# Idle TensorE products placed by the fill of a stretch instead of by single gaps, in a one-core block of attention, feed-forward and a state-space scan

## The reference, cut to what matters

```python
x = x + _L0_attn_a_ref(_layernorm(x, axis=-1), ...)   # 16 heads of 8, window of 32 and every 64th
x = x + _L0_ffn_ref(_layernorm(x, axis=-1), ...)      # 256 -> 512 -> 512 -> 128, weights +1 or -1
x = x + _L0_attn_b_ref(_layernorm(x, axis=-1), ...)   # 256 channels x 16 states, h = dA * h + dt * u * B
x = x + _L0_ffn_ref(_layernorm(x, axis=-1), ...)
```

## Time and profile before

| | |
|---|---|
| median of 3 runs | 799.41 us (798.85 to 801.1) |
| the profiled execution, its own time | 800.71 us |
| its span on the core | 798.9 us |
| busy PE, DVE, ACT, POOL | 89%, 86%, 77%, 75% of the span |
| mean granted TensorE clock | 0.981 |

### The profile page before, as it was taken

One profiled execution on the slowest core, in us unless ns is written; L12 is line 12 of the kernel. 1 busy time (PEld: TensorE's weight loads), 2 busy tenths in 40 slices (PEclk: granted clock), 3 DMA queues, 4 the chain that ended last, 5 costly groups with the idle time before them and its releaser, 6 DMA issues. The chain is left out here.

```text
span 798.9 us, 22483 instructions
## 1 busy us (share of the span) xinstructions
PE 710.9 (89%) x8144; PEld 420.1 (53%) x8144; DVE 689.1 (86%) x1145; ACT 617.5 (77%) x1227; POOL 601.3 (75%) x591
## 2 busy tenths in 40 slices
PE   7998998998789999999999998998998989697788
PEld 5675655645565446547555364445454555262346
DVE  6887127999999989999899989999999898798983
ACT  4775789889769998999689989887778656754533
POOL 3032345879988989769897799799798999898671
PEclk9999999999999999999999999999999999798989
DMA  6000019997987769786968799978897989899860
GB/s 204 3 3 2 2 45 244 255 236 224 269 218 198 176 173 270 202 216 184 232 185 237 215 241 255 229 222 242 222 248 215 269 245 256 225 244 255 213 156 27
DMA packets 84176, 154.95 MB, mean 194 GB/s; under 512 B 9433, under 2 KB 10082, under 8 KB 84066
## 3 DMA queue, kind: packets, MB, share of 16 engines
q1 hardware_dynamic: 84066, 153.51, 71.7%
HBM read 142.47 MB, written 11.01 MB: 192 GB/s over the span
## 5 line engine op out<-in xcount | busy, mean ns | idle before, releaser
L1752 POOL TENSOR_TENSOR d<-d,cr 128x1024 f32<-128x1024 f32 x128 | 300.4, 2354 | 34.1 <-DVE d L1264 24.4
L1574 ACT ACTIVATE ps<-dt,An 128x512 f32<-128x512 f32 x256 | 173.7, 690 | 53.6 <-DVE d L1264 39.8
L1264 DVE TENSOR_TENSOR_SCAN d<-ps,hl,d 128x512 f32<-128x512 f32 x128 | 157.8, 1267 | 8.6 <-ACT ps L1574 7.1
L1264 DVE TENSOR_TENSOR_SCAN d<-ps,d 128x512 f32<-128x512 f32 x128 | 150.5, 1206 | 7.4 <-ACT ps L1574 4.4
L877 PE MATMUL ps<-h,w 128*128 128x512 f16 (+1 forms) x512 | 121.8, 392 | 11.2 <-DVE h L1208 9.6
L1252 DVE TENSOR_TENSOR d<-ps,d 128x512 f32<-128x512 f32 x184 | 118.4, 673 | 2.1 <-DMA d<-dud 1.9
L1739 POOL TENSOR_TENSOR d<-d,br 128x512 f32<-128x512 f32 x72 | 91.4, 1276 | 13.2 <-DMA d<-dud 13.1
L877 PEld LDWEIGHTS ps<-h,w 128*128 128x128 f16 x512 | 49.1, 101 | 85.8 <-DVE h L1208 21.7
L951 PE MATMUL ps<-d,cst 128*32 128x512 f32 x512 | 70.5, 625 | 11.4 <-POOL d L1752 8.3
L815 PE MATMUL ps<-cst,sx 128*128 128x128 f32 x384 | 55.4, 279 | 10.9 <-ACT sx L1411 5.5
L888 PEld LDWEIGHTS ps<-w,h 128*128 128x128 f32 x496 | 56.7, 192 | 7.8 <-ACT h L1477 6.1
(11 more groups left out here) (177 smaller groups left out, 1337.7 us busy)
## 6 DMA issues: line engine op xcount, KB each, us to landing
dt<-dtd SPq DMA_DIRECT2D x256, 256.0 KB, 5.3
d<-dud SPq DMA_DIRECT2D x256, 256.0 KB, 5.3
dtd<-sR SPq DMA_DIRECT2D x16, 256.0 KB, 3.6
dud<-sE SPq DMA_DIRECT2D x16, 256.0 KB
X<-in_x SPq DMA_DIRECT2D x8, 256.0 KB, 6.1
br<-bcd SPq DMA_DIRECT2D x8, 256.0 KB, 3.3
cr<-bcd SPq DMA_DIRECT2D x8, 256.0 KB, 3.7
out<-X SPq DMA_DIRECT2D x3, 512.0 KB, 5.6
```

Of the source, the lines that this page charges most:

```text
L1264: eng.tensor_tensor_scan(d, banks[u % NG][:, :], d, hl[:, r:r + 1] if m % 2 else 0.0, ALU.mult, ALU.add).then_inc(v_sc, 1)
L1574: eng.activation(banks[u % NG][:, :], DT[:, u % NT, :], ACT.Exp, scale=An[:, g:g + 1]).then_inc(s_da, 1)
L1752: eng.tensor_tensor(d, d, CR[m % 2][:, :].unsqueeze(1).to_broadcast((128, n, 512)), ALU.mult).then_inc(p_cm, n)
```

## The change

Only the table `WARM` differs. Before, it had 33 rows with 176 products, now it has 48 rows with 276. Three rows are gone (1, 2 and 2 products, at 20307, 170847 and 214233), 18 are new, and 29 of the 30 that stay have one or two products more; the first stays at 8. The largest new rows are 20 products at 745957 and 6 at 718479. All other planned times are the same, so that on no engine do any other steps change their order.

```diff
 WARM = [
...
-    (765576, 5, 2),
+    (701632, 4, 10), (706498, 6, 7), (718479, 6, 6), (729975, 7, 3), (732272, 7, 5), (734105, 6, 3), (745957, 4, 20), (765576, 5, 4),
 ]
```

## The result

The changed kernel takes 809.18 us (median of 4 runs, 808.12 to 810.92) beside 799.82 for the kernel before on the same chip (4 runs, 798.85 to 801.1). The ratio is 1.0118, its 95% interval 1.0094 to 1.0143. The direction was forecast; the time was not: 804.8 us with a range to 807.5. The profiled execution took 809.81 us, its span is 808.0.

A forecast was written before the change was run, and what follows sets the result against it. With TensorE busy 89% and VectorE 86% of 798.9 us, no engine had room to spare for long. Terms 0.3 + 1.34 + 4.46 - 0.67 = 5.4 us gave 804.8 us for the median, range 800.2 to 807.5.

The forecast's parts named there:

- The 64 products: Products ahead of 718479: nearly all hidden in TensorE's idle time, 0.3 us in all, bounds 0 and 4.8 us.
- rival C: Slower: one in three of the 64 early products reaches the path, 809.2 us; chance 0.08.
- The 6 products: Between first and second `fl2_t` of (2, 2, 0): on TensorE's chain, 1.34 us whatever the low clock, bounds 0 and 2.8.
- The 20 products: Ahead of `csum_t(61)`, from 763.1 us: no idle time there, so all behind moves by 4.46 us.
- the 0.67 us of gain from the 6: The 20 start 1.34 us later, so less of them falls to the low clock, giving back 0.67 us.
- The clock: Last 130 us: the change earns no clock back; it falls in the same four places, 689.4 to 767.9 us.
- a sign of being wrong: Forecast is wrong if one of the four low-clock stretches from 689.4 to 767.9 us is gone.
- the price at the low clock: 0.47 us a product, from 16 passes taking 3.78 us near the kernel's start.
- The sum: Whole kernel: 5.4 us more, 806.1 us for the profiled execution and 804.8 us for the median.
- What would show it: Timeline signs, among them scan steps up to 720 us within 0.5 us of where they were.
- The range: 8 in 10 for the whole kernel's time: 800.2 to 807.5 us.

The follow-up runs named there:

- e9: Changed kernel plus 54 small products at 65676, without its late products except the 6 at 718479; 800.99 us, ratio 1.0017.
- e6: Changed kernel without the 13 products of rows 125534 and 127745; 811.73 us, ratio 1.0157.
- e5: Changed kernel plus 54 small products (216 instructions) at 65676; 806.07 us, ratio 1.0074.
- e4: Changed kernel with its rows up to 118115 as in the kernel before, ten products fewer; 806.2 us, ratio 1.0094.
- e1: Kernel before with only the new table's rows from 718479 on, 36 products more; 803.52 us, ratio 1.0059.
- e3: Changed kernel plus 24 small products (96 instructions) at 65676; 814.46 us, ratio 1.0185.
- e2: Kernel before plus ten small products (40 instructions) at 65676, in idle time; 803.55 us, ratio 1.0061.
- e7: Kernel before with only the row of 20 products at 745957 added; 803.29 us, ratio 1.0045.
- e10: Kernel before plus 64 small products (256 instructions) at 65676; 798.91 us, ratio 0.9989.
- e8: Kernel before with idle products added in the thin TensorE stretches of the last 130 us and inside `fl2_t`; 810.45 us, ratio 1.0128.

## Why the prediction was wrong, step by step

- **The 64 products: the step that failed.** It took the cost of a product as its own time on TensorE, less idle time, 0.3 us in all, and put both bounds by that. As far as the products themselves go it was right: in e9 all 64 and the 6, with the borders at 128 us moved back, gave a lateness of 0.6 us and a ratio of 1.0017 (1.0035 at most, 2.8 us). What the step left out is that each product is four instructions. Ten products ahead of 125 us moved a border to a place right behind a burst, which cost 4.9 us: 3.13 of standstill, and the rest from the low clock behind it, in which the 13 products of the next two rows ran (some 1.5 us by e6). The upper bound of 4.8 us was near this size by chance, and rival C's 809.2 us is the measured time by another mechanism: C had the products reach the path, and e5 and e9 show that they don't.
- **The trace of before had the sign.** Its timeline of TensorE has rows of equal passes cut in two, at 53, at 217 and at 351 us:

```profile
52.32 0.70 PE L832 MATMUL ps<-v,pt 128*32 128x18 f32 x51
53.82 0.61 PE L832 MATMUL ps<-v,pt 128*32 128x18 f32 x45 [0.80 <-issue]
...
350.32 0.65 PE L742 MATMUL ps<-cst,aT 128*64 128x128 f32 x7
351.72 0.76 PE L742 MATMUL ps<-cst,aT 128*64 128x128 f32 x9 [0.74 <-issue]
```

  The last is a standstill of the same kind (number 9153), and it ended 1.44 us behind a q8 packet's end at 350.28; the first is at 1985, 1.28 us behind a packet's end. The prediction didn't ask what "issue" was waiting for.
- **The 6 products: 1.34 us.** Right in e4, e5 and e6, where the lateness grows by 1.3, 1.2 and 1.2 us from 730 to 750 us. In the kernel after, e1, e3 and e9 it grows by 0.1 to 0.3 only. What differs is the low stretch: it starts 0.7 to 1.0 us behind the first `fl2_t` of (2, 2, 0) in before, e4, e5 and e6, and 1.0 to 1.6 us ahead of it in the other four, so that less of the second layer falls into it. But in these four the lateness grows ahead of the six by 0.5 to 1.4 us, from 690 to 720 us: in the kernel after by 1.4, where the low stretch lies at 696.1 and not at 689.4. Over 690 to 750 us the seven kernels with the six become later by 0.6 to 2.2 us (after: 1.8), and e2, e7 and e10, without them, by -0.1 to 0.2. So the size holds on the whole; the reasoning that the low clock doesn't matter here holds only where its stretch stays in its place. `fl2_s` waited 2.38 us, not 2.82 + 1.3.
- **The 20 products: 3.79 us.** Right: 3.85 in e4, 3.8 in e5 and e6, 3.3 in the kernel after, 3.2 in e1 and e3, and 4.4 alone (e7, where the 0.67 us of gain from the 6 can't arise). VectorE's wait ahead of `zs` grew from 1.34 to 3.97 us, by 2.6 and not by 4: its last `out_v` came later too, at 779.93.
- **The clock.** No stretch of the earlier trace rows was earned back, as said; two merged, which was named as a sign of being wrong. Outside the last 130 us, stretches came and went: 132.9 came with the standstill, 211.5 us came, and 453.8 went and gave 1.8 us back. The last is no effect of the change (e1, e7 and e8 lack it too); of 211.5 it isn't shown. One reading was wrong: the earlier trace rows were given as the price at the low clock, but the trace has no granted clock ahead of 10 us. The size holds all the same: 12 passes at 0.50 took 2.77 us in the kernel after, 0.46 us a product.
- **The sum.** 5.4 us was forecast and the trace of e4, the change without its ten early products, has 5.13: 806.6 against 806.1 us for the profiled execution. By its ratio e4 is 7.5 us over before (5.1 to 9.9), so the 5.4 is at the edge of what its runs allow. In the kernel after, the missing term is the standstill with the low clock behind it, 4.9 us. All else came to 4.2 us of the 9.1, for which 5.4 were forecast; the low clock at 453.8 us that this trace lacks makes it 1.8 lower.
- **What would show it.** "I am wrong ... if the scans at 700 us are already late by over 2 us": they are 3.9 us late at 700 us and 5.4 at 710.
- **The range** ended at 807.5, with rival C left out. The 100 products shift up to 415 records against 67 borders, and what such shifts do should have been in it: with the same late rows, kernels that differ in early instructions alone lie at 0.59% (e1), 0.74% (e5), 0.94% (e4), 1.18% (after), 1.57% (e6) and 1.85% (e3).

No kernel here is faster than the one before by more than a measurement tells.

## What to carry to other kernels

A product that is added to an engine's stream costs its time and its instructions. Where idle time on an engine is put down to nothing in the profile ("issue") and cuts a row of equal instructions in two, number the instructions and look whether the cuts are multiples of a fixed count apart, and whether an instruction packet ended just ahead. Before judging a reordering, pad the stream to a whole block: a loss that goes away with useless instructions is not one of the reordering; and a higher mean clock is no aim by itself (e8: 0.987, and 10 us slower).

## What the runs showed of the hardware

- TensorE's instructions come in packets of 16.4 KB for each 256, on the DMA engines that carry the data. Ahead of the standstills a packet took 0.9 to 1.7 us; the one ahead of the 3.13 us started 4.2 us behind the last border, and TensorE went on 1.24 to 1.52 us behind a packet's end. The standstills were 0.53 to 3.93 us long, at 192 above a multiple of 256 or one beyond, counted in the trace's records. They differ between executions of the same instructions (0.74 us and none at number 9153).
- Idle times of 0.6 to 0.7 us at two such numbers (2241 and 5312 in the kernel before) had no packet ending near them. They aren't standstills of this kind: the timeline gives VectorE's `jt` and ScalarE's `zn` as what TensorE waited for.
- A standstill can bring the low clock down on what is behind it: 3.4 us of it behind 3.13, 6.8 behind 2.59, 3.4 around 1.81, 10.2 around the two of e3, none behind 1.21 and 1.25. Idle products behind it then stand in the way: 12 passes took 2.77 us in place of 1.50.
